# A GNN stack on one core: the eight spline weights of an edge move from SBUF to a free PSUM bank

## The reference, cut to what matters

```python
w = jnp.where(bits_f[None] > 0, frac[:, None, :], 1.0 - frac[:, None, :])   # 3 coordinates, 8 corners
weights = jnp.prod(w, axis=-1)                                              # [E, 8]
xj = x[src]                                                                 # [E, 64]
z = (B[:, :, None] * xj[:, None, :]).reshape(Etot, S * x.shape[1])          # [E, 8 * 64]
msg = z @ W.reshape(S * x.shape[1], W.shape[2])
agg = jax.ops.segment_sum(msg, dst, num_segments=x.shape[0])
```

## Time and profile before

| | |
|---|---|
| median of three runs | 13193.13 us |
| the profiled execution: its time, its span | 13194.9 us, 13193.0 us |
| busy PE, DVE, ACT, POOL | 7957.6, 5160.7, 1792.7, 8307.1 us |
| granted TensorE clock, mean | 0.75 of 2.4 GHz |
| L1134 DVE, the product, x392 | 900.2 us, mean 2297 ns |
| L535 POOL, gathers from `spline_tab`, x1568 | 1984.8 us, mean 1266 ns |
| L535 POOL, gathers from `gat_tab`, x1568 | 1524.0 us, mean 972 ns |
| L511 POOL, scatters, x672 | 1202.0 us, mean 1789 ns |
| the spline pass | from 141 to about 3420 us |

### The profile page before, as it was taken

One profiled execution on the slowest core, in us unless ns is written; L12 is line 12 of the kernel. 1 busy time (PEld: TensorE's weight loads), 2 busy tenths in 40 slices (PEclk: granted clock), 3 DMA queues, 4 the chain that ended last, 5 costly groups with the idle time before them and its releaser, 6 DMA issues.

```text
span 13193.0 us, 199759 instructions
## 1 busy us (share of the span) xinstructions
PE 7957.6 (60%) x44286; PEld 5757.4 (44%) x44287; DVE 5160.7 (39%) x12670; ACT 1792.7 (14%) x4699; POOL 8307.1 (63%) x7522
## 2 busy tenths in 40 slices
PE   5878888888646666676666345534545345524445
PEld 5777888888534555555555111121112111101112
DVE  6545555555633333333334222232223222242223
ACT  0000011111123333333443000000000000000000
POOL 5788888777566666665442666646665566646664
PEclk9888899999767777788887566656666566656666
DMA  6111111111132222222221333323332232323332
GB/s 250 18 16 15 16 16 16 15 15 15 4 69 64 61 61 59 59 60 61 62 56 32 76 85 82 85 50 82 85 82 61 74 85 79 85 55 83 85 85 67
DMA packets 533179, 800.90 MB, mean 61 GB/s; under 512 B 319934, under 2 KB 329453, under 8 KB 532837
## 3 DMA queue, kind: packets, MB, share of 16 engines
q0 software_dynamic: 311952, 330.95, 14.0%
q1 hardware_dynamic: 218485, 466.48, 11.1%
q10 hardware_dynamic: 2400, 0.53, 0.0%
HBM read 700.08 MB, written 97.36 MB: 60 GB/s over the span
## 4 chain that ended last, share of the span: by engine, by line
issue 21%; DVEq 18%; PE 11%; another core or an unknown queue 10%; DVE 8%; ACT 3%; ACTq 1%; DMA 0%; POOL 0%; POOLq 0%; SPq 0%
DVEq L1329 4%; DVEq L1310 3%; DVE row_part L1310 3%; DVE R L1329 2%; DVEq L1325 2%; PE psAB L845 2%; PE psAB L851 2%; DVEq L357 2%; PE psCD L858 2%; DVEq L333 1%; DVEq L1305 1%; DVEq L1313 1%; DVEq L1309 1%; DVE A L1313 1%
## 5 line engine op out<-in xcount | busy, mean ns | idle before, releaser
L535 POOL DMA_INDIRECT gath<-sum_tab,idx_block x3584 | 3544.6, 989 | 2446.0 <-issue 1499.7
L885 PE MATMUL psAB<-gath,R 128*128 128x192 bf16 x4832 | 798.2, 308 | 3136.0 <-DVE R L1329 2351.8
L792 PE MATMUL psAB<-one_hot,R 128*128 128x128 f32 x15680 | 2322.2, 309 | 438.8 <-DVE one_hot L1105 322.5
L792 PEld LDWEIGHTS psAB<-one_hot,R 128*128 128x128 f32 x15680 | 2171.4, 214 | 482.8 <-issue 456.3
L535 POOL DMA_INDIRECT gath<-spline_tab,idx_block x1568 | 1984.8, 1266 | 615.4 <-issue 524.7
L535 POOL DMA_INDIRECT gath<-gat_tab,idx_block x1568 | 1524.0, 972 | 1336.2 <-DVEq L1038 897.6
L885 PEld LDWEIGHTS psAB<-gath,R 128*128 x4832 | 455.3, 102 | 3462.4 <-issue 3399.3
L1329 DVE SCALAR_TENSOR_TENSOR R<-iota_row,tile_base,dstf 128x512 f32 x1208 | 915.6, 758 | 2567.6 <-issue 2567.6
L511 POOL DMA_INDIRECT dense<-count_block,cell_block x672 | 1202.0, 1789 | 350.8 <-issue 187.4
L1134 DVE TENSOR_TENSOR R<-gath,R 128x2048 f32<-128x2048 f32 x392 | 900.2, 2297 | 413.0 <-DMA gath<-spline_tab,idx_block 398.1
L901 PE MATMUL psCD<-R,Q 128*128 128x512 f16 x1960 | 953.9, 487 | 42.1 <-issue 37.7
(11 more groups left out here) (251 smaller groups left out, 8922.3 us busy)
## 6 DMA issues: line engine op xcount, KB each, us to landing
R<-dense SPq DMA_DIRECT2D x280, 896.0 KB
Q<-dst_rows SPq DMA_DIRECT2D x392, 256.0 KB
dense<-stage SPq DMA_DIRECT2D x70, 896.0 KB
gath<-sum_tab,idx_block POOLq DMA_INDIRECT x3584
gath<-spline_tab,idx_block POOLq DMA_INDIRECT x1568
gath<-gat_tab,idx_block POOLq DMA_INDIRECT x1568
sum_tab<-Q SPq DMA_DIRECT2D x28, 672.0 KB, 5.5
dense<-count_block,cell_block POOLq DMA_INDIRECT x672
```

The lines of the kernel that those rows point to most:

```text
L535: nc.gpsimd.indirect_dma_start(out=dest[:, s, j, :], out_offset=None, in_=table, in_offset=bass.IndirectOffsetOnAxis(ap=idx_block[:, c:c + ...
L792: nc.tensor.matmul(block, z[:, w, j, k * P:(k + 1) * P], oh32[:, j, :], start=(j == 0), stop=(j == J - 1))
L885: ins = nc.tensor.matmul(psAB[:, ring(v, 0, SV, 512, 3 * F)], oh16[:, bass.ds((v & (SV - 1)) * GE + j * P, P)], gath_sum[:, s, j, :], star ...
```

## The change

`hat8` no longer lies in R, but in the first 32 columns of psB. R's layout closes the gap: what lay behind `hat8` (the cell lists `cell_a` and `times_a`) moves down by 32 columns. Nothing else is changed; the instructions, their order and their semaphores are the same.

```diff
         hat2 = R[:, o:o + 4 * J].rearrange("p (j a b) -> p j a b", a=2, b=2)
-        hat8 = R[:, o + 4 * J:o + 12 * J].rearrange("p (j a b) -> p j a b", a=2, b=4)
-        o += 12 * J
+        o += 4 * J
         cell_a, times_a = R[:, o:o + DC].bitcast(i32), R[:, o + DC:o + 2 * DC]
...
         psE = pb("psE", 1024)
+        hat8 = psB[:, 0:KS * J].rearrange("p (j a b) -> p j a b", a=2, b=4)
         ps_turned, ps_product = (psA, psB), (psCD, psE)
```

## The result

The changed kernel took 13677.74 us in the median of four runs, against 13196.0 for the kernel before on the same chip: a ratio of 1.0363, 95% interval 1.035 to 1.0376. I had forecast 12925 and a range up to 13080. It is slower by 3.6%, where I had put a chance of 0.05 on slower, and for another reason than the one I gave (a dearer product).

The account below looks back on a forecast made before the run. The prediction took POOL (GpSimd) to bound the spline pass's middle stretch, held by the product. Savings of 242 middle, 25 first and 0 last stretch make 267 us: 13193 − 267 = 12926, said as 12925, range 12780 to 13080.

Parts of the forecast that it names:

- GpSimd is no longer held: Spline pass: with the product's second operand in PSUM, gathers and scatters lose their held time, 350 us in the middle stretch.
- rival 1: Full gain: all stretches of the spline pass fall to POOL's need, 350 + 75 + 157 = 582 less, about 12610; chance 0.08.
- The product's own time: DVE's big product in each slot: stays at 2.29 us with one operand in PSUM, no gain.
- the writing of the weights: DVE's 32-element product L1129, one a slot, now ending in psB: 0 taken, at worst 39 us, no wait added.
- Rival 4: Slower: the product takes 4.42 us from PSUM reads at two cycles an element, about 13635; chance 0.05.
- Rival 3: GpSimd is still held, because the VectorE instruction's size and not its two SBUF inputs holds it: 13193; chance 0.07.
- rival 2: The two limits add: POOL's four-slot lead evens out little, single slots take 7.06 us, double ones 2 × 6.30; about 13130; chance 0.14.
- What is late next: Spline pass after POOL is freed: TensorE and DVE visits limit the gain to 242 us middle, 25 first, 0 last stretch.
- the last stretch's price: 6.30 us a visit, measured in the spline pass's last stretch, where the product never waits for rows.
- the dear end: Least gain in the spline pass, all visits at 6.30 us: 1789 us in the middle stretch, 359 in the first.
- the three stretches: Spline pass cut at 141.2, 504, 2491 and 3411 us: 56, 232 and 104 slots; 57, 284 and 146 visits.
- POOL's floor: GpSimd's own need without held time: 1637 us in the middle stretch (7.06 a slot), 288 in the first.

Follow-up runs that it names:

- f4: Changed kernel with one of a slot's four spline gathers, its rows read four times by the product; first kind of chip: 0.9419 of the kernel before, pass 2489 us.
- e1: Changed kernel with one 256-column fill (0.33 us) on GpSimd behind each spline gather; first kind of chip: 0.9854 of the kernel before, pass 3053 us.
- f5: Changed kernel with one fill on GpSimd behind each spline gather, run again in another set; first kind of chip: 0.9853 of the kernel before, pass 3048 us.
- e1b: Changed kernel with two fills on GpSimd behind each spline gather; first kind of chip: 1.0712 of the kernel before, pass 4164 us.
- e7: Changed kernel with spline gathers of 64 rows instead of 128; first kind of chip: 1.0364 of the kernel before, pass 3724 us.
- e8: Changed kernel with four fills together behind a slot's fourth gather; second kind of chip: 1.0259 of the kernel before, pass 3492 us.
- e10: Changed kernel with two instructions without work on GpSimd behind each spline gather; second kind of chip: 1.0429 of the kernel before, pass 3682 us.
- e12: Kernel before (weights in SBUF) with the slot given back right behind the product, before the visits; second kind of chip: 0.9998 of the kernel before, pass 3195 us.
- e5: Changed kernel with the slot given back right behind the product, before the visits; second kind of chip: 0.9534 of the kernel before, pass 2676 us.
- f1: Changed kernel unaltered, measured again as a control; first kind of chip: 1.0343 of the kernel before, pass 3699 us.
- e11: Changed kernel unaltered, measured again as a control; second kind of chip: 0.9528 of the kernel before, pass 2674 us.
- f2: Changed kernel with all spline weights zero; first kind of chip: 1.0331 of the kernel before, pass 3670 us.

## Why the prediction was wrong

*GpSimd is no longer held: right.* The gathers' mean fell from 1.266 to 0.956 us and the longest from 3.128 to 1.258, the scatters' from 1.789 to 1.700. POOL's busy time in the pass fell by 555 us, about the 350 + 75 + 157 of rival 1. Of the two versions of the Trainium skill's page "SBUF — State Buffer", section "Who interferes with whom", the trace agrees with the first (only two SBUF inputs block): 3.128 us against 1.258 for the same gathers.

*The product's own time, and the writing of the weights: right.* 2.286 us, and no wait is added. Rival 4, which ended near the measured time with 13635, is refuted in its mechanism. Rival 3 too. Of rival 2's sign, that the visits' gaps grow by what POOL gave back, the half on the gaps is there, but they grew by more, and not because a lead of four slots evens out little: the product never waits for rows.

*What is late next: wrong, and this is the step that failed.* I took the visit at "the last stretch's price", 6.30 us, as the dear end, made of "the slow clock level, second visits of a slot and gaps without a releaser, none of which the change touches". The change touched two of the three. The visits cost 7.53, 7.81 and 7.49 us on this chip, so the three stretches took 429, 2217 and 1094 us where I had summed 338, 1745 and 920. At 1.2 GHz the pass spends 1184 instead of 631 us; at 2.4 GHz it spends 2556 instead of 2638, so all that was lost lies in time at the slow level. The gaps without a releaser grew most: L1105's "remote" from 252.5 to 751.5, L1113's from 122.1 to 360.7, TensorE's own from 146 to 360.

How the one leads to the other: shown is that the signals come late under GpSimd's bursts (timeline, release instants), that taking gathers away takes the holds away (f4), and that spacing them does so in part (e1, f5: 169 and 147 us of holds) or in full (e1b, where GpSimd is the bound as well). GpSimd's busy time as such isn't what holds them, since e1 and e1b have more of it and fewer holds, nor are the bytes moved (e7). That time at 1.2 GHz goes with waiting, whatever the wait is for, is seen in e1b, e8 and e10: no holds, but 1140 to 1757 us in which the product waits for rows, and 775 to 1492 us at 1.2 GHz. That the late signals and TensorE's gaps cause the changed kernel's 1184 us in the same way is the reading that fits; no run separates the two, since f4 took away the holds, the gaps and the slow time together.

*The same prediction on the other kind of chip.* There it is 11365 − 533 = 10832. With no holds the visits cost 5.30, 5.73 and 5.10 us, and the middle stretch took 1627 us, where I had worked out POOL's floor as 1637; the first 302 (288) and the last 745 (920 − 157 = 763). That is rival 1, the full gain, to which I gave 0.08: 582 less by its sum. I had capped the gain by visits of 6.30 us, and that price held what was late or slow on my chip: with the weights in SBUF on the second kind (e12, as fast as the kernel before), a visit of the last stretch takes 873/146 = 5.98 us, of which 140.9/146 = 0.97 is the product's wait for rows, so about 5.0 without it. There the last stretch waited for GpSimd too, which is why it could gain. The rows are line L1113 and the product's wait of that stretch:

```profile
2465.00:3338.00 873.00, 31.80 (x146) 0.96 0.13 16
```

```profile
DVE R L1134 <- DMA gath<-spline_tab,idx_block: 140.9, 56, 5.5
```

The rows I had could have warned me: the kernel before already shows waits of VectorE and ScalarE ended by "remote" (L1105, 252.5 us), and I passed over a line that named no releaser as if it were a constant.

Still open: what differs between the two kinds of chip; through what the gathers hold TensorE's signals and open gaps in its work; whether two gathers in a row do it; and why the kernel before, with GpSimd busy 79% of the pass against 55%, has the fewer holds. That its held gathers leave a pause under each product, in which signals come through, fits the 48% above and e1's gain by added pauses, but it isn't shown.

No version was best on both kinds as far as run. One fill behind each gather (e1) is faster than the kernel before on the first kind, 0.985; on the second it wasn't run, and the milder two fills a slot gave 0.964 against 0.953 for the changed kernel alone.

## What to carry to other kernels

Freeing an engine that was the bound changes when its work falls, not only how much there is: ask what signals the other engines send during its bursts, and whether idle time in the trace that names no releaser may grow. Compare on more than one chip before explaining a few per cent, and run the changed kernel itself in each set; here the sign of the result depended on the kind of chip (1.036 and 0.953), and I read a cure (e5) into a difference of chips. A cap on a gain taken from a stretch of the same trace carries that chip's stalls in it.

## What the runs showed of the hardware

- Two kinds of chip: 12999, 13004 and 13196 us in three sets of runs of the kernel before, 11365, 11366 and 11366 in three others; behind the spline pass alone the changed kernel takes 9792 and 8024 us.
- On the first kind TensorE's signals can land up to 6.3 us (e7) behind the last recorded end of an L795 or L800, four or five of them 0.05 us apart, and in the changed kernel about half of the long ones within 1 us of the end of a burst of indirect DMAs on GpSimd (93 of 205; in f1 103 of 193). On the second kind they land 16 to 18 ns behind it.
- On the first kind TensorE also has gaps with no releaser between its matmuls: 360 us in the changed kernel's pass, none with one gather a slot (f4). On the second kind they are 0.4 us (e11).
- An indirect gather of 64 rows takes 916 ns of GpSimd, one of 128 rows 956.
- A VectorE product of 2048 elements a partition with one operand in PSUM, each word of it read 64 times, takes 2.286 us; with both in SBUF 2.292. Only with both in SBUF does it hold GpSimd's gathers (3.128 us at the longest, against 1.258).
- With the product's data all zero the holds are 557 us and the time at 1.2 GHz 1116 us (f2), against 574 and 1130 on the same chip (f1). Moving half the rows doesn't lessen them either: 695 and 1140 us (e7).
